# Norms in halves, earlier loads for layer 1, and a wide attention whose keys come turned by DMA

## The reference

```
x = x + L0_xattn(norm(x), ctx, mask)   16 heads of 8, biases
x = x + L0_ffn(norm(x))                ternary weights, 8-bit activations, 512 wide
x = x + L1_xattn(ctx, norm(x), mask)   latents norm(x), normed again inside; 2 heads of 64
x = x + L1_ffn(norm(x))                8 experts, 2 taken, 512 wide
x = x + L2_xattn(norm(x), ctx, mask)   16 heads of 64
x = x + L2_ffn(norm(x))                8 experts, 2 taken, 256 wide
x = x + L3_xattn(norm(x), ctx)         16 heads of 8
x = x + L3_ffn(norm(x))                ternary weights

L2_xattn:  xn = ln(x, ln1);  cn = ln(ctx, lnc);  q = xn @ Wq;  k, v = split(cn @ Wkv)
           k, v = concat(null, k), concat(null, v)       one extra key for each head
           attn = softmax(mask(q * 16**-0.5 @ k.T));  out = (attn @ v) @ Wo;  ln(out, lno)
```

## Time and profile before

| stage | from, us | to, us |
|---|---|---|
| L0a | 0 | 435 |
| L0f | 436 | 501 |
| L1a | 502 | 806 |
| L1f | 807 | 927 |
| L2a | 929 | 1808 |
| L2f | 1810 | 1884 |
| L3a | 1885 | 2309 |
| L3f | 2310 | 2361 |

### The profile page before, as it was taken

How to read it: one execution, slowest core, us unless ns; L and a number is a source line. 1 busy time by engine, 2 the same in 40 slices (tenths; PEclk the granted TensorE clock), 3 DMA queues, 4 the chain that set the end, 5 groups by cost and what they waited for, 6 DMA issues and landing times. The chain is left out here.

```text
span 2361.9 us, 48903 instructions
## 1 busy us (share of the span) xinstructions
PE 2141.9 (91%) x19446; PEld 1587.3 (67%) x19446; DVE 1444.6 (61%) x3160; ACT 1210.7 (51%) x2347; POOL 608.3 (26%) x233
## 2 busy tenths in 40 slices
PE   6999999448999697899999999999996889999995
PEld 3777777336888553577777777777773447777773
DVE  5777777568888344555544554455533667777775
ACT  5777787204666231244444444444430367777761
...
GB/s 168 141 148 136 140 151 87 14 79 78 128 114 72 19 36 62 42 17 18 29 22 17 17 24 27 17 18 17 1 1 10 44 154 141 133 145 124 126 63 17
DMA packets 87073, 165.20 MB, mean 70 GB/s; under 512 B 40384, under 2 KB 48624, under 8 KB 86592
## 3 DMA queue, kind: packets, MB, share of 16 engines
...
...
HBM read 81.75 MB, written 0.46 MB: 35 GB/s over the span
## 5 line engine op out<-in xcount | busy, mean ns | idle before, releaser
L1540 PEld LDWEIGHTS L2ps<-L2values,L2probsT 125*128 125x128 f32 (+1 forms) x2688 | 317.5, 192 | 50.6 <-issue 49.6
L1521 PE MATMUL L2ps<-L2keys,L2qz 128*128 128x501 f32 x672 | 340.0, 589 | 0.9 <-DVE L2out_bias L1784 0.9
L1540 PE MATMUL L2ps<-L2values,L2probsT 125*128 125x128 f32 (+1 forms) x2688 | 318.4, 275 | 0.0
L1737 DVE CUSTOM_DVE_ANT_0 L2work<-L2ps,L2maskadd,L2big 128x1503 f32<-128x1503 f32 x112 | 199.7, 1783 | 163.2 <-PE L2ps L1521 163.2
L122 POOL TENSOR_TENSOR rstd<-mv,half_neg 112x8 f32<-112x8 f32 x9 | 16.8, 1866 | 972.1 <-DVE mv L138 972.1
L1535 PEld LDWEIGHTS L2ps<-const,L2work 128*126 128x126 f32 x1344 | 163.8, 140 | 116.5 <-issue 64.9
L647 ACT ACTIVATE L3probsT<-L3ps 128x448 f32<-128x448 f32 x384 | 196.0, 547 | 70.8 <-PE L3ps L504 66.0
L647 ACT ACTIVATE L0probsT<-L0ps 128x448 f32<-128x448 f32 x384 | 198.1, 551 | 48.0 <-PE L0ps L504 46.8
L1535 PE MATMUL L2ps<-const,L2work 128*126 128x128 f32 x1344 | 202.2, 273 | 1.8 <-ACT L2work L1661 1.0
L1652 ACT ACTIVATE L2z<-L2ps,L2rinv 128x128 f32<-128x128 f32 x112 | 41.1, 367 | 304.8 <-PE L2ps L1540 304.8
L791 DVE TENSOR_REDUCE L3partmax<-L3ps 112x1 f32<-112x1000 f32 x128 | 153.4, 1198 | 58.3 <-PE L3ps L477 56.3
...
## 6 DMA issues: line engine op xcount, KB each, us to landing
L0key_stack<-L0key_parts SPq DMA_DIRECT2D x192, 187.5 KB
L3key_stack<-L3key_parts SPq DMA_DIRECT2D x192, 187.5 KB
L0ctxT<-in_ctxT SPq DMA_DIRECT2D x16, 750.0 KB, 4.2
L1raw<-in_ctx SPq DMA_DIRECT2D x16, 750.0 KB
L1rawT<-in_ctxT SPq DMA_DIRECT2D x16, 750.0 KB, 5.7
L2raw<-in_ctx SPq DMA_DIRECT2D x16, 750.0 KB
L3ctxT<-in_ctxT SPq DMA_DIRECT2D x16, 750.0 KB, 4.5
...
```

The source lines that it names most:

```text
L1521: last = nc.tensor.matmul(PS[:, 3 * (m % 2) + c, 0:NPR], tile_rows(m), KT[:, m // RT % 2, 500 * c:500 * c + NPR], start=True, stop=True)
L1540: last = nc.tensor.matmul(PS[:, bank, 0:P], PT[0:keys_in(c), i % 2, c, :], V[0:keys_in(c), i // RT % 2, c, :], start=c == 0, stop=c == NCH ...
L1737: nc.vector.tensor_tensor_reduce(SM[:, m % 2, :].rearrange("p (c n) -> p c n", c=3), PS[:, 3 * (m % 2):3 * (m % 2) + 3, 0:NPR], MA[:, m // ...
```

## The change

1. Every norm at a stage's start is done in two halves of four tiles, each with its own waits; the double norm of L1a and L2a is one pass, with variance * (1 + e2) + e1 * e2 in the power.
2. `LatentAhead`: L1a's weights, and the raw context, turned context and mask of batches 0 and 1, are loaded during L0f. In L1a, units K and V of batch 0 stand behind the matmuls of the latents' q and k, those of batch 1 behind scores of tile 0; two copies move from VectorE to ACT; statistics of batch 0 come after the norm; `deviations(1)` comes after the first key norm on POOL.
3. `WideAhead`: L2a's weights are loaded in L1f; the weights' scaling goes to POOL there, in pieces of four heads behind the gates, as do the powers of the context's variances. VectorE keeps a sum and a bias for each of two weights, in experts 5 and 6.
4. L2a's loop: probabilities are multiplied by the reciprocal of their sum on VectorE before PE turns them (`scale`), O is computed with features on partitions by swapping its operands, so that ACT copies it straight to its place, and unit Z goes. Keys of batches 1 to 15 are not turned by PE: the turned context comes by DMA, 112 rows and 15 rows; mean and reciprocal deviation of each key are spread over 128 partitions by two DMAs from a scratch in DRAM; POOL subtracts and multiplies.
5. Two nested scopes in `build` hold what the two Ahead classes keep, and each ends with one more clearing of semaphores.

```diff
@@ ln_dve
+    for h in range(2):
+        tiles = range(4 * h, 4 * h + 4)
+        dve.wait_ge(s.ln_tok, h + 1)
+        for t in tiles:
             last = nc.vector.bn_stats(k.stats[:, t, :], src(t))
...
+            last = nc.vector.tensor_scalar(var, var, 1.0 + eps[1], eps[0] * eps[1], ALU.mult, ALU.add)
+        last.then_inc(s.ln_var, 1)
...
+    for h in range(2):
+        dve.wait_ge(s.ln_rstd, h + 1)
...
@@ latent_units
-    units = kv(0, (0, 1)) + kv(0, (2,)) + kv(1, (0, 1)) + kv(1, (2,)) + turned_keys(0)
+    units = kv(0, (0, 1, 2)) + turned_keys(0) + kv(1, (0, 1, 2))
@@ WideAhead, new
+    def gpsimd(self, pool):
+        nc, s = self.nc, self.s
+        pool.wait_ge(s.w_loaded, 64)
+        pool.wait_ge(s.rows_loaded, 48)
+        for n in (1, 2):
+            for g in range(4):
...
+                nc.gpsimd.tensor_tensor(self.products[:, n - 1, heads], w, row(1), ALU.mult).then_inc(s.products, 1)
+                pool.wait_ge(s.products, 4 * n + g - 3)
+                nc.gpsimd.tensor_tensor(w, w, row(0), ALU.mult).then_inc(s.scaled, 1)
+                pool.wait_ge(s.scaled, 4 * n + g - 3)
+                nc.gpsimd.tensor_tensor(w[:, :, 0:P - 1], w[:, :, 0:P - 1], w[:, :, P - 1:P].to_broadcast([64, 4, P - 1]),
+                                        ALU.subtract).then_inc(s.centred, 1)
+        pool.wait_ge(s.ve_ready, 1)
+        for b in range(B):
+            nc.gpsimd.tensor_tensor(self.rs[:, b, :], self.rs[:, b, :], self.k.half_neg[0:CH, 0:NCH], ALU.pow).then_inc(s.spread, 1)
@@ attention_16_wide_heads, SP
+            def load_keys(b):
+                if b == 1:
+                    sp.wait_ge(s.slot_ready, 2)
+                    sp.wait_ge(s.q_filled, 2 * H)
+                else:
+                    sp.wait_ge(s.scores_filled, RT * (b - 1))
+                    sp.wait_ge(s.keys_scaled, b - 1)
+                for rows in (slice(0, TT), slice(TT, P - 1)):
+                    sp.dma_start(KT[rows, b % 2, 0:S2], src["ctxT"][b][rows]).then_inc(s.key_parts, 16)
+                for x, to in enumerate((MEAN[:], SCALE_OF)):
+                    sp.dma_start(to, scratch[x, b].rearrange("c n -> (c n)").partition_broadcast(P)).then_inc(s.key_parts, 16)
@@ PE
+                    elif m % RT == 0:
+                        pe.wait_ge(s.keys_scaled, m // RT)
...
-                        pe.wait_ge(s.exp_done, i + 1)
+                        pe.wait_ge(s.scaled, i + 1)
...
-                        last = nc.tensor.matmul(PS[:, bank, 0:P], PT[0:keys_in(c), i % 2, c, :], V[0:keys_in(c), i // RT % 2, c, :],
+                        last = nc.tensor.matmul(PS[:, bank, 0:P], V[0:keys_in(c), i // RT % 2, c, :], PT[0:keys_in(c), i % 2, c, :],
...
@@ POOL
+            for b in range(1, B):
+                pool.wait_ge(s.key_parts, 64 * b)
+                nc.gpsimd.tensor_tensor(KT[0:P - 1, b % 2, 0:S2], KT[0:P - 1, b % 2, 0:S2], MEAN[0:P - 1], ALU.subtract
+                                        ).then_inc(s.keys_moved, 1)
+                pool.wait_ge(s.keys_moved, b)
+                nc.gpsimd.tensor_tensor(KT[0:P - 1, b % 2, 0:S2], KT[0:P - 1, b % 2, 0:S2], SCALE_OF[0:P - 1], ALU.mult
+                                        ).then_inc(s.keys_scaled, 1)
@@ ACT
-                    ins = nc.scalar.mul(ZB[:, g, t % 4, :], PS[:, bank, 0:P], rinv[:, i % 4:i % 4 + 1])
+                    ins = nc.scalar.copy(tile_rows(i), PS[:, bank, 0:P])
@@ DVE
+            def scale(m):
+                dve.wait_ge(s.exp_done, m + 1)
+                nc.vector.reciprocal(rinv[:, m % 4:m % 4 + 1], ssum[:, m % 4:m % 4 + 1]).then_inc(s.rinv_ready, 1)
+                dve.wait_ge(s.rinv_ready, m + 1)
+                nc.vector.tensor_scalar(PR[:, m % 2, :], PR[:, m % 2, :], rinv[:, m % 4:m % 4 + 1], None, ALU.mult
+                                        ).then_inc(s.scaled, 1)
...
+            scale(0)
             for n in range(plan.last_step + 1):
...
                 if t in (1, 2, 3) and b + 1 < B:
                     normalise(b + 1, t - 1)
+                if n + 1 < RT * B:
+                    scale(n + 1)
                 if n + 2 < RT * B:
                     maximum(n + 2)
```

More of the change, by code:

```diff
@@ L1077, in _ @@
             scores(0, range(4))
+            for j in range(3):
+                unit("K", 1, j)
+                unit("V", 1, j)
             for n in range(B):
@@ L1333, in _ @@
             last.then_inc(s.lat_done, 1)
-            empty("K", 1, 2)
             empty("T2", 0, 1)
+            maximum(0)
+            for j in range(3):
+                empty("K", 1, j)
             stats(2)
@@ L1374, in __init__ @@
         for n in range(self.last_step + 1):
-            self.units += [u for u in (self.first(n), self.second(n), self.extra(n), self.third(n), self.output(n)) if u]
+            self.units += [u for u in (self.first(n), self.second(n), self.third(n), self.output(n)) if u]
         self.place = {u[:3]: i for i, u in enumerate(self.units)}
@@ L1600, in _ @@
                     unit(*plan.second(n))
-                if plan.extra(n):
-                    unit(*plan.extra(n))
-                if ahead:
+                if more:
                     scores(n + 2, 1)
```

419 lines of the change are left out of this document (208 added, 211 removed).

## The result

The changed kernel takes 2279.22 us (median of four runs, 2278.47 to 2282.62) where the one before takes 2363.66 (2362.05 to 2366.44, four runs beside it): 0.9644 of the time, 95% interval 0.9628 to 0.9661. Forecast were 2292 us in 2278 to 2318. The gain is 84.4 us against 71.8 forecast: the direction was right, and most of the places; the forecast was 12.6 us short of the gain, and the measured time lies 1.2 us inside the low end of the range.

What follows compares the result with a forecast made beforehand. PE was taken to bound layer 2's wide attention loop (busy 766.89 of 770.00 us), with short serial stretches elsewhere. Terms of -31.8, +4.5, +2.1, -1.7, -20.8, -14.7, -10.2 and +0.8 sum to -71.8 from 2363.66: 2292 us, range 2278 to 2318.

Steps and rivals of the forecast that it cites:

- The loop's transposes: L2a's loop: Z units and PE's key transposes of batches 1 to 15 go, -31.8 us.
- The lock: L2a's loop: POOL's key instructions block VectorE's two-port instructions, 0.3 us for each of 15 batches, +4.5 us.
- The rival of both instructions on one multiplication: L2a's loop: both POOL instructions of a batch block the same VectorE multiplication, +26 us, 2313; chance 0.18.
- The forecast's third bound: L2a's loop: both POOL instructions block one multiplication in a step that also normalises, 3.8 us a batch, +57.
- Start of L2a: PE no longer waits for VectorE's weight folding, moved to POOL in L1f; q starts earlier, -20.8 us, bounds -12 and -24.
- The loop's start: L2a's loop: tile 0's multiplication stands behind tile 1's maximum, delaying the transposes, +2.1 us, bounds 2.1 and 2.9.
- Norms in halves: Norms opening stages, and L2a's last: halves overlap statistics, power and copy; together -14.7 us, bounds -8 and -19.
- L1a: Start of L1a: early loads, single-pass double norm and copies on ACT bring T2(1) to 564.3, -10.2 us.
- POOL in L1f: POOL finishes 24 folding pieces at 1.1 us and 16 powers near 896, before L2a begins at 928.9.
- Late keys: L2a's loop: key chain of 78 us misses its 48.5 us window, +442, about 2734 us; slower case, chance 0.04.
- the broadcasts at the mask's rate: L2a's loop: the two 750 KB key broadcasts take 34 us each if as slow as the mask's 187.5 KB in 8.5.
- more than I count: Rival for the whole kernel: no lock cost (-4.5) and L1a at -15.4, giving 2282 us; chance 0.19.

Runs made afterwards that it cites:

- the loads asked for three steps later: Changed kernel with each batch's key loading asked for three steps later, so POOL's two instructions fall into steps where VectorE normalises values; 2330.01 us.
- the folding in whole weights: Changed kernel with POOL's folding of layer 2's weights in L1f in 6 instructions of 64x2048 instead of 24 of 64x512; 2286.36 us.
- PE kept busy in the norms: Changed kernel with 16 more PE transposes into an unread bank in L1f, L2a's last norm, L2f and L3f; 2285.57 us alone.
- the folding on VectorE: Changed kernel with layer 2's weight folding back on VectorE in L2a, eight instructions of 64x2048, loads still early, powers in L1f; 2302.09 us.

## Why the prediction was right, and where it was short

**The loop's transposes** (-31.8): right. From the first transposes of tile 0 to the last norm the loop took 786.0 us before and 754.8 after, -31.2, which also holds the last Z unit's -1.7, the lock's cost and 1.6 us of slower first steps.

**The lock** (+4.5, bounds 0 to +57): the bound 0 it is. What failed is the 0.3 us for each batch: it took one blocked operation to cost up to 0.4 and POOL's start to be "at a random point". Loading starts at a fixed step, the chain from issue to finished keys is 16.4 to 18.9 us long (forecast 16), and in the loop POOL's pair always starts between 0.1 us ahead of step 6 and 2.3 us into it, two steps and more behind the last that normalises; the slack there covered every struck multiplication, of up to 4.16 us. The rival of both instructions on one multiplication falls by the trace (VectorE is let in between them). Its price was also wrong as added up: 2 x 3.02 less the slack of 2.8 is 3.2 us a batch, +49, and not 1.7 and +26, and 2336 would have been outside the range. The forecast's third bound, 3.8 us a batch where the step also normalises, is near what the loads asked for three steps later measured (3.6 a batch, clock included). The Trainium skill ("SBUF — State Buffer", "Who interferes with whom") has an exclusive lock held for a whole instruction; the 3.16, 7.30 and 7.33 us agree.

**Start of L2a** (-20.8): -28.3 up to the first scores (43.8 us for 72.0). This is the term that was mis-sized, by 7.5 of the 11 us that L2a gained beyond the forecast: 5.4 up to q and 2.1 in its making. The working took PE's folding and turn at their durations before, 7.19 and 1.76 us, which were those of half clock; they took 3.83 and 1.2. Where the clock did fall (the folding in whole weights), q began at 11.0 us, the low end of the "about 11 to 13" that I forecast, and the scores 5.0 us later than in the changed kernel: so about 5 of the 7.5 are the clock.

Why it stayed up is open. That the wait of 19.58 us had brought it down before, and its going kept it up, does not fit the trace of the kernel before, where the first transposes of the stage, ahead of that wait, already ran at half clock (columns as in the loop's row, granted clock 0.50):

```profile
928.88:930.81 1.93, 1.93 (x8) 1.51 (x8) 0.26 (x1) 0.00 (x0) 0.42 (x4) 0.50 0.43 72
```

The clock had fallen 0.8 us ahead of them, as it does 0.7 us ahead with PE kept busy in the norms, where no such wait follows; it falls 1.6 us behind the stage's start with the folding in whole weights and 2.3 with the folding on VectorE. In the changed kernel and in seven experiments that leave L1f and the norms alone it holds until 39.7 or 39.8 us. In the two kernels that wait there the clock stays low longer, 37.5 us before and 27.3 with the folding on VectorE, against 17.1 and 13.7 in the two without the wait. What in L1f decides where the fall comes is not shown either; in the 10 us ahead of the stage PE is busy for 7.05 in all of them.

**The loop's start** (+2.1): the wait came as worked out (3.09 for 1.03); one more effect, 1.6 us of slower first steps, was covered by faster scores ahead of it.

**Norms in halves** (-14.7): -16.8 over the same stages, a barrier's 0.4 in it, L3f's two (-4.0 for -2.9) the largest miss. Taken out alone they cost 27 us, 9.0 of it in L2a, most at its start, outside this term. **L1a** (-10.2): -11.2 with a barrier's 0.4 in it, T2(1) forecast at 564.3 and found at 563.4. **POOL in L1f**: forecast done 33 us before L2a, found 30, with pieces of 1.0 to 1.3 us, one of 1.5 and one of 1.6 among them, where 1.1 was used.

**Late keys** (the slower case): chain at most 18.9 us, window 48.6. Its doubt, the broadcasts at the mask's rate, falls by 6.8 and 8.9 us to landing.

Nearly all misses lie on one side, so they add up (start of L2a 7.5 us, lock 4.5, norms 2.5, L1a 1.4, less 2.0 of L0a and 0.9 of the loop and its start): the time is beyond the rival "more than I count" (2282), and for another reason than that one gave. The lock did cost nothing, but L1a came out at -11.2 and not -15.4; the rest was the start of L2a, for which the forecast had -24 as its bound and the trace -28.3. That the time still fell inside the range is in part luck.
